# Attention over two batches as one program: the second batch's input and the first batch's output are normalised in pieces beside the pairs

## The chip, the cores and the metric

The kernel runs on one core of one Trainium2 chip. The metric is the device time of one execution in microseconds (us). A core has five engines that run their own instruction streams and wait for each other on semaphores: TensorE (PE; its weight loads are listed as PEld), VectorE (DVE), ScalarE (ACT), GpSimd (POOL), and SyncE (SP), which here only issues DMAs.

## The reference, cut to what matters

Two batches of 2048 tokens with 128 channels pass through four layers, each followed by `layernorm(x + layer(x))`: a state-space layer, a quantised linear layer, attention, and a mixture of experts. The change is in the third:

```python
mu = jnp.mean(latents, axis=-1, keepdims=True)
var = jnp.mean((latents - mu) ** 2, axis=-1, keepdims=True)
x = (latents - mu) * jax.lax.rsqrt(var + 1e-05) * ln_gamma + ln_beta
q = (x @ Wq) ...; k = (x @ Wk) ...; v = (x @ Wv) ...      # 16 heads of 64
scores = jnp.einsum('bhqd,bhkd->bhqk', q * scale, k * scale)
weights = jax.nn.softmax(scores, axis=-1)
out = jnp.einsum('bhqk,bhkd->bhqd', weights, v)
return out @ Wo
...
x = _layernorm(x + _L1_attn_ref(x, ...), axis=-1)
```

No token of one batch attends to the other batch, so the batches are independent.

## The kernel before, in words

`phase1` (the first two layers), `phase2` (attention) and `phase3` (experts) run one after the other. `phase2` runs four programs for batch 0 and then the same four for batch 1, with a barrier of all engines behind each:

- `attention_input` loads the 2048 tokens, normalises them (statistics on DVE, roots on ACT, scaling on both), turns them on PE (L951, 16 transposes of 128x128) and leaves them in `xaT` with gamma and beta applied.
- `attention_first` makes keys, queries and values of the first pair of heads, and the row maxima of its first scores.
- `attention_pairs` is the long one. Heads are taken in 8 pairs, queries in 4 chunks of 512. A **group** `g` is one pair and one chunk (32 groups per batch; `GC`), and its 16 key tiles are **units** `(g, kt)`. Groups are cut in 4 **turns** of 4 units (`TURNS`, `TURN`).
- `attention_output` finishes the last group, turns `attnT` back to tokens (L1493), adds the residual, normalises and stores.

Per unit in `attention_pairs`: PE computes two heads' scores in four terms (L1249) into one of two double banks; ACT takes their exponential into one of ten buffers `p` (`weigh`, L1356, `LIVE = 10`); PE multiplies them with the values (`values`, L1262); POOL adds up the denominators (L1389, 15 adds of 128x1024 per group, each waiting for the one before). ACT may fill a buffer of `p` again only when both PE and POOL have read what it held ten units earlier. Beside that, PE computes raw scores of groups ahead (L997), of which DVE takes row maxima (L1441) for the softmax shift. Only the group's last raw scores decide its shift (L1011 to L1013, turned by L1021, copied by ACT at L1329).

Each turn has two places for a further job, `USES_AT`, before and behind its four `values` steps: projections of the pair ahead, the denominator (`den`), the output projection (`out`), the shift. The place behind turn 3 is free:

```python
USES_AT = {(0, "before"): 0, (0, "behind"): "values", (1, "before"): "den", (2, "before"): "out",
           (2, "behind"): "shift", (3, "before"): 1}
```

A job's result lies in one of three banks used in turn (`TURNING`), shared with the raw scores. The third item behind a job waits until ACT (for a job behind) or DVE (before) has read it. At a turn's start ACT reads what was made behind the turn before; at turn 0 it then copies the finished group out of PSUM (`copy_outputs`, L1347, once per group), and takes four exponentials.

Jobs for the pair ahead exist only while there is one: in the last four groups of a batch there are no projections, and in the last two none or fewer raw scores.

## Time and profile before

| what | value |
|---|---|
| median of 3 runs | 3673.57 us (3668.96 to 3675.05) |
| the profiled execution's own time | 3673.23 us |
| its span, first to last instruction | 3671.3 us |
| busy, share of the span: PE | 3307.6 us, 90% |
| PEld | 1789.2 us, 49% |
| DVE | 2405.5 us, 66% |
| ACT | 1717.1 us, 46% |
| POOL | 2757.9 us, 75% |
| granted TensorE clock, mean | 0.954 of full speed |

An engine's share is a mean over stages that have different limits. A query for a stretch gives the same numbers for that stretch alone. In a timeline row the columns are start, duration, engine, line, operation, output<-inputs, count, and in brackets the idle time of the engine before it with what ended it.

### The profile page before, as it was taken

To read this page: it belongs to the slowest core of one execution; us is meant where nothing else is said; L and a number is where in the kernel's file an instruction comes from. 1 tells how busy PE (TensorE), PEld (TensorE's weight loads), DVE (VectorE), ACT (ScalarE), POOL (GpSimd) and SP (SyncE) were. 2 spreads that over 40 slices of the span, in tenths; PEclk is the share of its full clock that TensorE was granted. 3 is DMA by queue.
4 is the path that set the end of the run, shared out by engine and by line. 5 is a ranking of instruction groups with operands and counts; after the bars stand their busy time and mean duration, and the time that the engine had idled before them with its cause. 6 is when DMAs were issued, how large, how long until landed. Compare 5 with 4: busy or idle time off the path is not lost. (4 is left out here: it accounts for less than half of the span.)

```text
span 3671.3 us, 52128 instructions
## 1 busy us (share of the span) xinstructions
PE 3307.6 (90%) x19957; PEld 1789.2 (49%) x19957; DVE 2405.5 (66%) x3711; ACT 1717.1 (47%) x2081; POOL 2757.9 (75%) x1153
## 2 busy tenths in 40 slices
PE   5776587479999999999999499999999999997898
PEld 2223232245555555555555255555555555553798
DVE  5898599766666666666664466666666666663554
ACT  3331433135555555555555245555555555553554
POOL 1784088249998998998999378998998998997233
PEclk9898789789999999999999799999999999999999
DMA  1331133110000000000000100000000000000000
GB/s 25 132 109 35 47 128 109 30 44 1 4 1 4 1 4 4 1 4 1 2 1 1 41 3 1 4 4 1 4 1 4 1 4 2 1 1 12 27 18 15
DMA packets 61411, 76.31 MB, mean 21 GB/s; under 512 B 7274, under 2 KB 48820, under 8 KB 61108
## 3 DMA queue, kind: packets, MB, share of 16 engines
q1 hardware_dynamic: 59362, 72.71, 6.1%
q8 instruction: 156, 2.56, 0.3%
q14 instruction: 83, 0.68, 0.1%
q10 hardware_dynamic: 1810, 0.37, 0.0%
HBM read 66.24 MB, written 6.82 MB: 20 GB/s over the span
## 5 line engine op out<-in xcount | busy, mean ns | idle before, releaser
L1389 POOL TENSOR_TENSOR den_g<-den_g,p 128x1024 f32<-128x1024 f32 x896 | 2133.8, 2381 | 222.4 <-ACT p L1356 109.5
L1441 DVE TENSOR_REDUCE quarters<-psum 128x1 f32<-128x512 f32 x1960 | 1262.1, 686 | 732.0 <-PE psum L997 679.3
L1356 ACT ACTIVATE p<-psum 128x1024 f32<-128x1024 f32 x1024 | 1025.2, 1026 | 502.4 <-PE psum L1249 470.9
L1262 PE MATMUL psum<-p,v 128*64 128x512 f32 x4096 | 923.3, 593 | 0.0
L1262 PEld LDWEIGHTS psum<-p,v 128*64 128x64 f32 x4096 | 292.2, 137 | 579.3 <-issue 569.5
L997 PE MATMUL psum<-k_main,q_main 64*128 64x512 f32 x2048 | 438.7, 423 | 13.7 <-DVE quarters L1004 11.1
L1249 PE MATMUL psum<-q_main,k_main 64*128 64x512 f32 x2048 | 436.1, 421 | 7.1 <-PEq L1137 4.9
L1249 PE MATMUL psum<-q_rest,k_main 64*128 64x512 f32 x2048 | 407.4, 393 | 0.0
L1249 PE MATMUL psum<-q_main,k_rest 64*128 64x512 f32 x2048 | 407.0, 392 | 0.0
L1249 PE MATMUL psum<-row_shift,row_ones 64*128 64x512 f32 x2048 | 406.7, 391 | 0.0
L736 POOL TENSOR_TENSOR seen<-state,c_sb 128x2048 f32<-128x2048 f32 x64 | 285.4, 4461 | 68.5 <-DVE state L683 60.3
L997 PEld LDWEIGHTS psum<-k_main,q_main 64*128 64x128 f32 x2048 | 206.0, 185 | 222.0 <-issue 136.7
L621 PE MATMUL psum<-seen,ident 128*128 128x512 f32 x512 | 264.5, 654 | 27.2 <-POOL seen L736 27.0
L1249 PEld LDWEIGHTS psum<-q_main,k_main 64*128 64x128 f32 x2048 | 193.5, 185 | 167.1 <-ACT p L1356 128.4
L1249 PEld LDWEIGHTS psum<-row_shift,row_ones 64*128 64x128 f32 x2048 | 194.9, 185 | 44.5
L1249 PEld LDWEIGHTS psum<-q_main,k_rest 64*128 64x128 f32 x2048 | 194.5, 185 | 44.8
L1249 PEld LDWEIGHTS psum<-q_rest,k_main 64*128 64x128 f32 x2048 | 194.6, 186 | 11.5
L723 POOL TENSOR_TENSOR xnT<-dx,work 128x1024 f32<-128x1024 f32 x32 | 75.3, 2352 | 158.3 <-DMA work<-bc_rows 158.3
L1389 POOL TENSOR_TENSOR den_g<-p 128x1024 f32<-128x1024 f32 x64 | 152.4, 2381 | 46.6 <-ACT p L1356 46.6
L1329 ACT CAST row_shift<-psum 2x512 fp32r<-2x512 f32 x124 | 71.5, 577 | 243.5 <-PE psum L1021 242.0
L621 PEld LDWEIGHTS psum<-seen,ident 128*128 128x128 f32 x512 | 95.9, 201 | 153.3 <-issue 103.6
L1846 POOL TENSOR_TENSOR mixed<-mixed,part 128x512 f32<-128x512 f32 x56 | 74.1, 1324 | 104.2 <-DVE part L1811 104.2
(260 smaller groups left out, 3327.0 us busy)
## 6 DMA issues: line engine op xcount, KB each, us to landing
c_sb<-bc_rows SPq DMA_DIRECT2D x64, 512.0 KB, 3.5
work<-bc_rows SPq DMA_DIRECT2D x32, 512.0 KB, 4.9
resid<-in_resid SPq DMA_DIRECT2D x8, 256.0 KB, 3.6
x_mid<-resid SPq DMA_DIRECT2D x8, 256.0 KB, 2.6
xa<-x_mid SPq DMA_DIRECT2D x8, 256.0 KB, 3.7
x_tok<-x_mid SPq DMA_DIRECT2D x8, 256.0 KB, 3.8
x_mid<-x_tok SPq DMA_DIRECT2D x8, 256.0 KB, 2.7
x<-x_mid SPq DMA_DIRECT2D x8, 256.0 KB, 2.8
```

The lines of the kernel that those rows point to most:

```text
L621: last = nc.tensor.matmul(y_sum[:, h, k * BANK:(k + 1) * BANK], ident[:], seen[:, i % SLOTS, h, k * BANK:(k + 1) * BANK], start=False, sto ...
L723: nc.gpsimd.tensor_tensor(fed[:, k % SLOTS, :], dx[:, 1, s * SCAN:(s + 1) * SCAN], b_sb[:, k % SLOTS, :], ALU.mult).then_inc(fed_by_pool, 1)
L736: nc.gpsimd.tensor_tensor(seen[:, i % SLOTS, 0:halves], state[:, i % SLOTS, 0:halves], c_sb[:, i % C_SLOTS, :].unsqueeze(1).to_broadcast([ ...
L997: last = nc.tensor.matmul(to[h], q[hi(h), c * BANK + j * P:c * BANK + (j + 1) * P], k[hi(h), piece(quarter)], start=True, stop=True)
L1249: last = nc.tensor.matmul(s_bank(u)[:, piece(h)], left[hi(h)], right[hi(h)], start=(i == 0), stop=(i == len(terms) - 1))
L1262: last = nc.tensor.matmul(o_bank[hi(h), :], vv[:, kt, hi(h)], p[:, u % LIVE, h, :], start=(kt == 0), stop=(kt == KT - 1))
L1329: nc.scalar.copy(row_shift[at:at + 2, (g + 1) % 2, :], bank[at:at + 2, :]).then_inc(shift_read, 1)
L1356: nc.scalar.activation(flat(p[:, u % LIVE]), s_bank(u), ACT.Exp, scale=float(DH) ** -0.5).then_inc(p_ready, 1)
L1389: nc.gpsimd.tensor_tensor(sums, first, src, ALU.add).then_inc(added_g, 1)
L1441: nc.vector.reduce_max(quarters[:, to % 2, h, n:n + 1], bank_of["max", u, h], X_AXIS).then_inc(max_read, 1)
L1846: nc.gpsimd.tensor_tensor(mixed[:, u % 2], x[:, u % 2] if e == 0 else mixed[:, u % 2], part[:, e % 2], ALU.add).then_inc(summed, 1)
```

## The change

`attention_pairs` now runs once, for 64 groups of both batches (`GC` = 64, `NEXT` = 32 is the first group of batch 1). The programs `attention_output` of batch 0, `attention_input` of batch 1 and `attention_first` of batch 1 are gone, with the barriers between them. `xaT` holds both batches, and the projections and raw scores for batch 1's first pair become ordinary jobs of groups 28 to 31. What the three programs computed besides is done in eight pieces of 512 tokens: four `input` pieces (batch 1) with the statistics in groups 22 to 25, and four `output` pieces (batch 0) with the statistics in groups 31 to 34. The loads of the tokens stand on SP ahead of all weight loads. Among the jobs, `input` and `output` first stand in the code of PE (transposes behind turn 3), then in that of ACT (the read at the next turn's start); `rough_root` and `normalise_tokens` are ACT's at the end of turn 2, `variance`, `refine` (six operations on 128x4, each waiting for the one before) and `add_residual` POOL's, `statistics` DVE's at the end of turn 0. Core of the diff:

```diff
+    ALL_PAIRS = BATCH * PAIRS
+    GC, NEXT = ALL_PAIRS * CHUNKS, PAIRS * CHUNKS
+    batch_of = lambda g: g // NEXT
+    jobs = [("input", c, NEXT - 10 + c) for c in range(CHUNKS)] + [("output", c, NEXT - 1 + c) for c in range(CHUNKS)]
+    job_at = {start: j for j, (_, _, start) in enumerate(jobs)}
...
+            if (i % TURNS, place) == (TURNS - 1, "behind"):
+                if NEXT - 9 <= g < NEXT - 9 + CHUNKS:
+                    uses.append(("input", g - (NEXT - 9), i, place))
+                elif NEXT - 3 <= g < NEXT - 3 + CHUNKS:
+                    uses.append(("output", g - (NEXT - 3), i, place))
...
+                for c in range(CHUNKS):
+                    sp.dma_start(tok[:, c], tokens(x_in, 1, c)).then_inc(x_loaded, 16)
+                for c in range(CHUNKS):
+                    sp.dma_start(residual[:, c], tokens(x_in, 0, c)).then_inc(residual_loaded, 16)
...
+                    if pair == PAIRS:
+                        for c in range(CHUNKS):
+                            sp.wait_ge(tok_normed, CHUNKS + c + 1)
+                            sp.dma_start(tokens(x_out, 0, c), tok[:, c]).then_inc(stored, 16)
...
+                    if what == "input":
+                        pe.wait_ge(tok_normed, g + 1)
+                        for j in range(TPC):
+                            last = nc.tensor.transpose(bank[:, j * P:(j + 1) * P], tok[:, g, j, :], ident[:])
+                    elif what == "output":
+                        pe.wait_ge(freed_by_vector, freed(use_of["out", NEXT - CHUNKS + g]))
+                        for j in range(TPC):
+                            last = nc.tensor.transpose(bank[:, j * P:(j + 1) * P], attnT[:, (g * TPC + j) * P:(g * TPC + j + 1) * P], ident[:])
...
+                    elif what == "input":
+                        nc.scalar.activation(xaT[:, 1, piece(g)], bank, ACT.Identity, scale=gamma[:, 0:1], bias=beta[:, 0:1]).then_inc(freed_by_scalar, 1)
+                    elif what == "output":
+                        nc.scalar.copy(tok[:, g].rearrange("p t d -> p (t d)"), bank).then_inc(tok_copied, 1)
+                        act.wait_ge(tok_copied, g + 1)
+                        nc.scalar.nop().then_inc(freed_by_scalar, 1)
...
+                def rough_root(j):
+                    var, root = (factors[:, j, k, :] for k in range(2))
+                    act.wait_ge(var_ready, j + 1)
+                    nc.scalar.activation(root, var, ACT.Ln).then_inc(rough, 1)
+                    act.wait_ge(rough, 2 * j + 1)
+                    nc.scalar.activation(root, root, ACT.Exp, scale=-0.5).then_inc(rough, 1)
+                def normalise_tokens(j):
+                    act.wait_ge(refined, j + 1)
+                    c = jobs[j][1]
+                    for t in range(TPC):
+                        last = nc.scalar.activation(tok[:, c, t, :], tok[:, c, t, :], ACT.Identity, scale=factors[:, j, 1, t:t + 1],
+                                                    bias=factors[:, j, 3, t:t + 1])
+                    last.then_inc(tok_normed, 1)
...
+                def variance(j):
+                    pool.wait_ge(stats_done, j + 1)
+                    nc.gpsimd.tensor_scalar(factors[:, j, 0, :], two_t[:, j, :, 1], EPS, None, ALU.add).then_inc(var_ready, 1)
+                def refine(j):
+                    var, root, t, offset = (factors[:, j, k, :] for k in range(4))
+                    pool.wait_ge(rough, 2 * (j + 1))
+                    st.link(nc.gpsimd.tensor_tensor(t, root, root, ALU.mult))
...
+                    nc.gpsimd.tensor_scalar(offset, offset, -1.0, None, ALU.mult).then_inc(refined, 1)
...
+                def add_residual(c):
+                    pool.wait_ge(tok_copied, c + 1)
+                    pool.wait_ge(residual_loaded, 16 * CHUNKS)
+                    nc.gpsimd.tensor_tensor(tok[:, c], tok[:, c], residual[:, c], ALU.add).then_inc(tok_added, 1)
...
+                    if kt == 6 and g in job_at:
+                        variance(job_at[g])
+                    if kt == 1 and g - 1 in job_at:
+                        refine(job_at[g - 1])
+                    if kt == 4 and NEXT - 2 <= g < NEXT - 2 + CHUNKS:
+                        add_residual(g - (NEXT - 2))
...
+                def statistics(j):
+                    for t in range(TPC):
+                        last = nc.vector.bn_stats(six_t[:, t, :], tok[:, c, t, :])
+                    last.then_inc(stats_step, 1)
+                    dve.wait_ge(stats_step, j + 1)
+                    for t in range(TPC):
+                        last = nc.vector.bn_aggr(two_t[:, j, t, :], six_t[:, t, :])
+                    last.then_inc(stats_done, 1)
```

**PE, where the batches met.** Before, PE had these rows between batch 0's last values (`p_0`) and batch 1's first raw scores; the branches are ends of programs, where the barriers stand:

```order
L1262 MATMUL psum<-p_0,v 64x512 x8
L1197 UNCONDITIONAL_BRANCH
L1482 UNCONDITIONAL_BRANCH
L1485 MATMUL psum<-den_g,ones 64x512 x2
L1493 MATMUL psum<-ident,attnT 128x128 x12
L1490 MATMUL psum<-o_raw,w_o 128x512
L1493 MATMUL psum<-ident,attnT 128x128 x4
L1471 UNCONDITIONAL_BRANCH
L945 UNCONDITIONAL_BRANCH
L951 MATMUL psum<-ident,xa_1 128x128 x16
```

Of the change, the same engine at the end of turn 3 of group 32, the last of the four `output` pieces; L1031 is the job before the values, L1293 the values, L996 and L1280 the next group's raw scores and scores:

```order
L1031 MATMUL psum<-xaT,w_qkv 64x512 x2
L1293 MATMUL psum<-p,v 64x512 x8
L1309 MATMUL psum<-ident,attnT 128x128 x4
L996 MATMUL psum<-k_main,q_main 128x512 x2
L1280 MATMUL psum<-q_main,k_main 128x512 x2
```

The 16 transposes of `xa` and the 16 of `attnT` moved from the stretch between the batches to eight places of four, each behind the values of turn 3.

**ACT, in a group with an input piece.** Of the change, group 23 from the exponentials of turn 2 on (L1402 is before's L1356, L1375 its L1329, L1393 its L1347):

```order
L1402 ACTIVATE p<-psum 128x1024 x4
L1408 ACTIVATE factors<-factors 128x4
L1410 ACTIVATE factors<-factors 128x4
L1417 ACTIVATE tok<-tok,factors 128x128 x4
L1375 CAST row_shift<-psum 2x512 x2
L1402 ACTIVATE p<-psum 128x1024 x4
L1382 CAST q_main<-psum 128x512
L1367 ACTIVATE xaT<-psum,beta,gamma 128x512
L1393 COPY o_raw<-psum 128x512
```

Before, the row of L1329 stood directly behind that of L1356, and that of L1347 directly behind the cast of `q_main`: the three rows on `factors` and `tok` and the one on `xaT` are new there.

**POOL, in group 32 or 33, where most of it comes together.** Of the change (L1480 is before's L1389):

```order
L1480 TENSOR_TENSOR den_g<-p 128x1024
L1454 TENSOR_TENSOR factors<-factors 128x4
L1455 TENSOR_TENSOR factors<-factors 128x4
L1456 TENSOR_SCALAR factors<-factors 128x4
L1457 TENSOR_TENSOR factors<-factors 128x4
L1458 TENSOR_TENSOR factors<-two_t,factors 128x4
L1459 TENSOR_SCALAR factors<-factors 128x4
L1480 TENSOR_TENSOR den_g<-den_g,p 128x1024 x3
L1465 TENSOR_TENSOR tok<-tok,residual 128x512
L1480 TENSOR_TENSOR den_g<-den_g,p 128x1024 x2
L1448 TENSOR_SCALAR factors<-two_t 128x4
L1480 TENSOR_TENSOR den_g<-den_g,p 128x1024 x9
```

Before, a group was one row of `den_g<-p` and one of `den_g<-den_g,p` x14: seven operations on 128x4 and one on 128x512 now stand between its adds.

## Rows read from the trace of the kernel before

**Rows 1.** The page's busy time by engine.

```profile
PE 3307.6 (90%) x19957; PEld 1789.2 (49%) x19957; DVE 2405.5 (66%) x3711; ACT 1717.1 (47%) x2081; POOL 2757.9 (75%) x1153
```

**Rows 2.** Stretches: length, busy (count) of PE, PEld, DVE, ACT, POOL, clock, DMA share, GB/s.

```profile
829.00:1893.62 1064.62, 1064.59 (x7130) 561.89 (x7132) 691.85 (x1107) 560.34 (x649) 964.72 (x406) 1.00 0.01 2
1893.62:2034.34 140.72, 139.59 (x892) 71.04 (x892) 70.03 (x109) 72.38 (x81) 131.77 (x57) 1.00 0.00 1
2034.34:2120.71 86.37, 33.10 (x188) 17.07 (x188) 51.71 (x133) 21.78 (x44) 14.38 (x8) 0.72 0.15 43
```

**Rows 3.** Timeline of ACT: the copy that ends groups 0, 27, 31, 32.

```profile
829.00 0.59 ACT L1347 COPY o_raw<-psum 128x512 f32<-128x512 f32 x1 [2.85 <-PE psum L1262]
...
1893.62 0.59 ACT L1347 COPY o_raw<-psum 128x512 f32<-128x512 f32 x1 [2.85 <-PE psum L1262]
...
2034.34 0.58 ACT L1347 COPY o_raw<-psum 128x512 f32<-128x512 f32 x1 [2.56 <-PE psum L1262]
...
2162.97 0.59 ACT L1347 COPY o_raw<-psum 128x512 f32<-128x512 f32 x1 [2.85 <-PE psum L1262]
```

**Rows 4.** Timelines of PE, POOL and DVE at the join.

```profile
2030.64 3.65 PE L1262 MATMUL psum<-p,v 128*64 128x512 f32 x16
2045.05 1.97 PE L1485 MATMUL psum<-den_g,ones 128*64 128x512 f32 x4 [10.76 <-PEq L1457]
...
2082.52 3.55 PE L951 MATMUL psum<-ident,xa 128*128 128x128 f32 x16 [29.41 <-DVE xa L121]
...
2009.11 34.95 POOL L1389 TENSOR_TENSOR den_g<-den_g,p 128x1024 f32<-128x1024 f32 x14
...
2075.32 3.19 DVE L104 BATCH_NORM_STATS2 six<-xa 128x6 f32<-128x128 f32 x16 [11.94 <-DMA xa<-x_mid]
```

**Rows 5.** Timeline of PE: the first matmul of turns 1, 2, 3 of a group.

```profile
1233.58 0.50 PE L997 MATMUL psum<-k_main,q_main 64*128 64x512 f32 x2
...
1243.17 0.51 PE L997 MATMUL psum<-k_main,q_main 64*128 64x512 f32 x2
...
1252.98 0.50 PE L997 MATMUL psum<-k_main,q_main 64*128 64x512 f32 x2
```

**Rows 6.** Timeline of PE in the experts: four transposes, what follows.

```profile
3519.31 0.60 PE L1617 MATMUL psum<-ident,x 128*128 128x128 f32 x4
3519.75 1.95 PE L1660 MATMUL psum<-down_w,hid 128*128 128x128 f32 x16
```

**Rows 7.** Timeline of POOL in the same group.

```profile
1225.69 9.95 POOL L1389 TENSOR_TENSOR den_g<-den_g,p 128x1024 f32<-128x1024 f32 x4 [1.53 <-ACT p L1356]
1236.15 25.13 POOL L1389 TENSOR_TENSOR den_g<-den_g,p 128x1024 f32<-128x1024 f32 x10 [0.52 <-ACT p L1356]
```

**Rows 8.** Groups of POOL: count, busy us, mean ns.

```profile
L1044 POOL TENSOR_TENSOR q_rest<-raw,q_main 128x512 fp32r<-128x512 f32 x8 | 10.2, 1272 | 86.2 <-ACT raw L1110 86.2
L159 POOL TENSOR_TENSOR stat<-stat,exponent 128x4 f32<-128x4 f32 x8 | 8.2, 1021 | 5.4 <-DVE stat L1770 4.6
```

**Rows 9.** DVE: one timeline row, two groups, one line's min/median/max ns.

```profile
1234.12 2.68 DVE L1441 TENSOR_REDUCE quarters<-psum 128x1 f32<-128x512 f32 x4 [3.42 <-PE psum L997]
...
L104 DVE BATCH_NORM_STATS2 six<-x_tok 128x6 f32<-128x128 f32 x32 | 7.0, 280 | 0.3
L1011 DVE TENSOR_REDUCE maxima<-quarters 128x8 f32<-128x32 f32 x64 | 11.4, 178 | 0.1
...
L1013 DVE TENSOR_TENSOR shift<-maxima,shift x64: 195/769/2278, 777.3 to 3326.4; 128x8 bf16<-128x8 f32 x64
```

**Rows 10.** ACT: two timeline rows of turn 3, two of before's normalisation.

```profile
1253.09 1.18 ACT L1329 CAST row_shift<-psum 2x512 fp32r<-2x512 f32 x2 [3.94 <-PE psum L1021]
...
1257.03 1.94 ACT L1356 ACTIVATE p<-psum 128x1024 f32<-128x1024 f32 x2 [0.40 <-PE psum L1249]
...
2060.08 0.22 ACT L153 ACTIVATE stat<-stat 128x16 f32<-128x16 f32 x1
2061.37 3.18 ACT L131 ACTIVATE x_tok<-x_tok,stat 128x128 f32<-128x128 f32 x8 [1.08 <-DVE stat L118]
```

More of the change, by code:

```diff
@@ L1286, in use @@
                             pe.wait_ge(weights, 48 * (g // CHUNKS))
-                        last = project(nc, bank, w, xaT, projection(what, g))
+                        last = project(nc, bank, w, xaT[:, batch_of(g + CHUNKS)], projection(what, g))
                     last.then_inc(use_full, 1)
@@ L1455, in _ @@
                         make_shift(nc, st, quarters[:, (g + 1) % 2], maxima[:], shift).then_inc(shift_ready, 1)
+                    if i % TURNS == 0 and g in job_at:
+                        statistics(job_at[g])
                 dve.wait_ge(freed_by_vector, sum(place == "before" for *_, place in uses))
```

57 lines of the change are left out of this document (41 added, 16 removed).

## The prediction

> **What bounds the kernel now.** I read the page's busy time first: PE is busy in 90% of the span, POOL in 75%, no other engine in more than 66% [rows 1]. Then the same by stretch. From the end of group 0 to the end of group 27 PE works 1064.59 of 1064.62 us at a granted clock of 1.00, POOL 964.72 [rows 2]. That is the attention proper, and PE bounds it. The reader should see that the stretch between the batches is another thing: in 86.37 us PE works 33.10 and is granted 0.72 of its clock [rows 2], which is a mean over stretches at the 2.4 and at the 1.2 GHz level. So I looked for what stands there and for how long a group takes elsewhere.
>
> ACT copies each group out once, at a fixed place, so those copies are a ruler. Group 0's starts at 829.00 and group 27's at 1893.62: 27 intervals of 39.43 us [rows 3]. The last four groups of the batch take 2034.34 - 1893.62 = 140.72, or 35.2 each, since they have no pair ahead to prepare. Then 128.63 us pass until group 32, the first of batch 1, is copied at 2162.97 [rows 3].
>
> The timelines show the chain in between. PE finishes its values at about 2034.3, but POOL still adds until 2009.11 + 34.95 = 2044.06, and the next program's first matmul is at 2045.05. Batch 1's statistics start at 2075.32 behind an 11.94 us wait for a load, and its first transposes at 2082.52 behind 29.41 us without PE work [rows 4]. It is all latency in series: no engine is full.
>
> **The sum, made against the profiled execution's 3673.23 us** (span 3671.3 and 1.93 around it; the median of the runs, 3673.57, is 0.34 more).
>
> *Removed.* From group 27's copy to group 32's: 2162.97 - 1893.62 = 269.35 us [rows 3]. In the changed kernel this is five ordinary groups, since each now has the next pair to prepare: 5 x 39.43 = 197.15. The difference is **72.20 us**. It is less than the 89.20 us that the one interval across the join loses (128.63 - 39.43), because groups 28 to 31 grow from 140.72 to 157.72: the first pair's projections and raw scores of batch 1 move into them at PE's full rate.
>
> *Transposes on PE.* 32 transposes are no longer in the removed stretch but in eight places of four. Four of them between other matmuls put the next one 0.44 us later in the experts (3519.31 to 3519.75) [rows 6]. As a check on such a place: turn 1, with nothing behind its values, takes 1243.17 - 1233.58 = 9.59 us, turn 2, with eight small matmuls there, 9.81 [rows 5]. The lower bound for a place is that 0.22. For the upper I take 1.0, twice the transpose price and a little, as if the switch from the values' matmuls and back cost as much again. I take 0.44, the same operation and shape: 8 x 0.44 = **3.5 us** (1.8 to 8).
>
> *ACT at turn 0.* It reads the piece (0.59 us, the time of the copy of the same shape [rows 3]) ahead of the group's copy and four exponentials. It sits idle 2.85 us ahead of that copy [rows 3], but waits there for the values, behind which the new transposes come. So the read does not go into that idle time but into the gap before the first exponential, which waits for PE's scores. PE's scores of a unit wait for the exponential two units before, so what ACT loses there PE loses. I think about 0.1 us per piece is left over, **0.8 us** for eight; from 0 to the whole read, 4.7.
>
> *ACT at the end of turn 2.* Two root steps (0.22 each [rows 10]) and four scalings (eight take 3.18, so four 1.6 [rows 10]): 2.0 us in groups 23 to 25 and 32 to 34, less in the others. ACT sits idle 3.94 us there, waiting for the shift [rows 10]. Hidden, at nothing. Without that cover it would be 2.0 us a piece, 16 us; queued behind it are the shift's copy and the exponentials of turn 3, for which PE waits.
>
> *DVE.* Four statistics (mean 0.280) and four small aggregations, about 1.2 us by the rows' kind [rows 9], at the end of turn 0, where DVE sits idle 3.42 us until the first raw scores of turn 1 [rows 9]. Nothing.
>
> *POOL.* This is the engine that could come to bind. Ten adds take 25.13 us, 2.51 each with the wait for the one before; 15 are 37.7 of the 39.43 us, so 1.7 us are free per group [rows 7]. The change puts in up to seven operations on 128x4 and one on 128x512 (1.27 us [rows 8]). No row has a plain 128x4 operation on POOL. From below: 2.38 us for 1024 columns (2.51 less the wait of 0.13) and 1.27 for 512 give about 0.17 for none, with the wait 0.3. From above: the power on 128x4, 1.02 [rows 8], with the wait 1.15. It is a costlier function than a multiply, so I take the lower end: 7 x 0.3 + 1.4 = 3.5 us in the worst groups, 32 and 33. Less the free 1.7 POOL falls 1.8 us back in each, some 4 us over the output pieces, 1 over the input pieces. What may it fall back? The second exponential of the row at 1257.03, at about 1258.0, comes ten units after the one that the second add of the row at 1236.15 reads, so it fills the same buffer; that add is over at 1241.2, 17 us earlier [rows 7, 10]. So no wait of ACT on POOL: nothing.
>
> *DMAs on SP.* Eight loads of 256 KB ahead of the pair weights, four stores between two weight loads. At before's join four such loads had landed by 2075.32. A pair's weights are first used four groups, some 158 us, after their load is issued. Nothing.
>
> *A rule against the trace.* L1013, a DVE operation of 8 columns with two SBUF inputs, takes 195 ns at best and up to 2278; L1011 of the same place, with one SBUF input, has a mean of 178 [rows 9]. Beside POOL's adds the one kind is held up and the other not. The Trainium skill (SBUF — State Buffer, section Who interferes with whom) says why: a VectorE instruction with two SBUF inputs contends with a GpSimd one that reads SBUF, and the later waits for the whole of the other; with one SBUF input and outside the two-port modes it does not. By that rule the statistics, with one SBUF input, run free and the sum stays at 3605; if they were held up like L1013, the sum would be that of rival 3.
>
> **Sum:** 3673.23 - 72.20 + 3.5 + 0.8 = 3605.3, I say **3605 us**, 1.9% less. With the bounds above for transposes and reads: 3602.8 to 3613.7.
>
> **The rivals.**
>
> 1. *POOL's small operations cost what the power costs.* For: the only 128x4 row there is, 1.02 us [rows 8]. Against: the intercept of the adds. Then a group with variance and refinement has 8.05 us more work and 1.7 free, so POOL falls back about 6.3 us a group. ACT's root step waits for the variance, ready some 10 us ahead of it now (the add behind which it stands ends at 1238.7, ACT's turn 2 ends about 1249.2 by the 3.94 us idle before 1253.09 [rows 7, 10]). In the third input piece POOL is some 17 us late at that place; less 10 and less ACT's spare 2, ACT stops PE for 5 to 6 us, and in groups 33 and 34 again. About 18 us: **3623**. Chance 0.10.
> 2. *ACT's part of a piece is not hidden.* Read and end of turn 2 both push the exponentials: 0.59 + 2.0 = 2.6 us a piece, 8 pieces 21 us, less the 0.8 counted: **3625**. For: PE waits for exponentials all the time by a few tenths, and ACT had idle time only in pieces. Against: the 3.94 us. Chance 0.08.
> 3. *The statistics are held up by POOL's adds; this one ends slower.* Place: DVE, end of turn 0, with PE's raw scores waiting for DVE behind it. Price: each of eight operations waits out an add, 2.51 us: 20.1 + 1.2, less the cover of 3.4, is 17.9 a piece and 143 for eight: **3748**. At L1013's mean delay (a median of 0.77 against 0.195: 0.6) it is 8 x 0.6 + 1.2 - 3.4 = 2.6 a piece, 21 us and still a gain. It decides from 68 / 8 = 8.5 us a piece, 10.7 us over the eight, 1.3 us for each operation. For: L1013. Against: L1011. Chance 0.03 for slower, 0.02 for the mild form, about 3626.
> 4. *The join does not go away:* the new program waits at group 32 for something of batch 1 (a weight load, a piece of `xaT`), so that a good part of the 72 us comes back. Against: each piece is ready a full turn before PE asks for it, the last piece of `xaT` at turn 0 of group 27, a group ahead of the first projection. 30 us back would be **3635**. Chance 0.02.
>
> **How the numbers follow.** Forecast 0.75. The range takes in its bounds, 3602.8 to 3613.7, then the scatter of the three runs (about 3 us to either side), and reaches some way to rivals 1 and 2: 3600 to 3618; outside it I leave rivals 1 to 4 and little of the forecast, 2 in 10 or a bit more. Within 0.2% (7 us, about what a measurement of this kernel can tell from no change) nothing ends: 0.01. Slower 0.03, faster 0.96.
>
> **What the changed profile would show.** Copies of `o_raw` 39.4 us apart through groups 28 to 36, those with a piece at 39.9 to 40.0, a clock of 1.00 throughout. Four transposes in 0.4 us. DVE's statistics of 0.28 each and the first maximum of turn 1 not later than before against PE. POOL's 128x4 operations of 0.15 to 0.3 us; if they take 1 us, rival 1. ACT idle before L1375 down from 3.94 to about 2; if zero, rival 2. The forecast is wrong if intervals beside the pieces grow by more than 1 us, or if any interval between groups 27 and 36 stands out by itself.

## The result, and the profile after

The changed kernel's median is **3606.24 us** (four runs, 3603.16 to 3610.68), against 3672.99 (four runs, 3668.96 to 3675.05) for the kernel before: a ratio of **0.9821**, 95% interval 0.9803 to 0.9838. Its profiled execution took 3604.98 us, with a span of 3602.7. In a later comparison it was 3605.48 (five runs) against 3669.22 (nine), again 0.9821 [0.9806, 0.9835].

The page's busy time by engine answers to [rows 1]:

```profile
PE 3297.9 (92%) x19959; PEld 1785.3 (50%) x19959; DVE 2405.3 (67%) x3701; ACT 1723.8 (48%) x2110; POOL 2768.0 (77%) x1209
```

Every engine has about as much to do as before; the span around the work is what shrank. The stretches by engine (columns as in [rows 2]) run from group 0's copy to group 22's, on to group 27's (input pieces), from group 28's to group 33's (output pieces), and across the former join, 27 to 32:

```profile
829.29:1696.37 867.08, 866.97 (x5810) 457.51 (x5812) 565.27 (x910) 456.71 (x531) 786.09 (x332) 1.00 0.01 3
1696.37:1895.80 199.43, 199.41 (x1338) 105.50 (x1340) 132.26 (x229) 113.53 (x146) 183.77 (x103) 1.00 0.01 2
1935.23:2134.78 199.55, 199.53 (x1338) 105.40 (x1340) 135.60 (x229) 110.03 (x138) 184.66 (x95) 1.00 0.02 5
1895.80:2096.02 200.22, 200.21 (x1344) 106.19 (x1346) 133.38 (x222) 108.19 (x133) 183.63 (x87) 1.00 0.02 5
```

Across the join PE now works 200.21 of 200.22 us at a granted clock of 1.00. The 86.37 us stretch with 33.10 us of PE work and a clock of 0.72 [rows 2] has no counterpart. The ruler, that is ACT's copy of a finished group [rows 3], on the changed kernel's timeline, groups 0, 22, 27, 32 and 33:

```profile
829.29 0.59 ACT L1393 COPY o_raw<-psum 128x512 f32<-128x512 f32 x1 [2.85 <-PE psum L1293]
...
1696.37 0.59 ACT L1393 COPY o_raw<-psum 128x512 f32<-128x512 f32 x1 [2.85 <-PE psum L1293]
...
1895.80 0.59 ACT L1393 COPY o_raw<-psum 128x512 f32<-128x512 f32 x1 [2.85 <-PE psum L1293]
...
2096.02 0.59 ACT L1393 COPY o_raw<-psum 128x512 f32<-128x512 f32 x1 [0.17 <-ACT tok L1369]
...
2134.78 0.59 ACT L1393 COPY o_raw<-psum 128x512 f32<-128x512 f32 x1 [2.85 <-PE psum L1293]
```

From group 27's copy to 32's are 200.22 us where 269.35 stood. All intervals, read off the same copies in both traces:

| intervals (us) | before | after |
|---|---|---|
| mean of groups 0 to 22 | 39.43 | 39.41 |
| 22 to 27, each | 39.42, 39.44, 39.45, 39.46, 39.38 | 40.69, 39.97, 40.03, 40.00, 38.74 |
| 27 to 28 | 36.89 | 39.43 |
| 28 to 33, each | 36.72, 35.92, 31.19, 128.63, 39.41 | 40.79, 39.99, 40.02, 39.99, 38.76 |
| last copy to the end | 302.72 | 302.57 |

The first interval with a piece is longer and the one behind the last shorter for a reason of the ruler: ACT reads the piece ahead of the copy (`[0.17 <-ACT tok L1369]` in the row at 2096.02), so the mark itself moves. Over five intervals that cancels: 199.43 and 199.55 us, against 5 x 39.41 = 197.07. Four input pieces cost 2.4 us and four output pieces 2.5. In the first interval the growth is 1.28 us (40.69 - 39.41), of which 0.68 is the moved mark (ACT's read of the piece starts at 1776.35 in the rows below, the copy at 1777.03) and 0.60 the piece.

Where the 68.6 us of span went, by these marks: 69.1 gained between the copies of 27 and 32 (269.35 - 200.22), 2.3 lost to the input pieces (199.43 against 197.15 before), 0.65 gained in the interval from 32 to 33, which is 67.5; the other 1.1 is the ordinary group, shorter by some 0.02 us more than fifty times over, and the ends.

The four engines in a group with an input piece, one place each: PE's transposes and the first matmul of the next turn behind them; ACT at the end of turn 2 and its read at turn 0; DVE at the end of turn 0.

```profile
1775.66 0.66 PE L1304 MATMUL psum<-ident,tok 128*128 128x128 f32 x4
1776.24 0.50 PE L996 MATMUL psum<-k_main,q_main 64*128 64x512 f32 x2
```

```profile
1762.15 0.19 ACT L1408 ACTIVATE factors<-factors 128x4 f32<-128x4 f32 x1
...
1762.49 1.63 ACT L1417 ACTIVATE tok<-tok,factors 128x128 f32<-128x128 f32 x4
...
1766.19 1.18 ACT L1375 CAST row_shift<-psum 2x512 fp32r<-2x512 f32 x2 [2.06 <-PE psum L1020]
...
1776.35 0.78 ACT L1367 ACTIVATE xaT<-psum,beta,gamma 128x512 f32<-128x512 f32 x1 [3.43 <-PE psum L1304]
1777.03 0.58 ACT L1393 COPY o_raw<-psum 128x512 f32<-128x512 f32 x1
1777.71 2.19 ACT L1402 ACTIVATE p<-psum 128x1024 f32<-128x1024 f32 x2
```

```profile
1743.75 0.86 DVE L1541 BATCH_NORM_STATS2 six_t<-tok 128x6 f32<-128x128 f32 x4
1744.64 0.38 DVE L1545 BATCH_NORM_AGGREGATE two_t<-six_t 128x2 f32<-128x6 f32 x4
1747.25 2.67 DVE L1555 TENSOR_REDUCE quarters<-psum 128x1 f32<-128x512 f32 x4 [2.23 <-PE psum L996]
```

Four transposes put the next matmul 0.58 us later (0.59 in the output piece at 2014.56). ACT's wait for the shift fell from 3.94 us [rows 10] to 2.06: it ends at PE's moment, not at ACT's. DVE's wait for turn 1's first raw scores fell from 3.42 [rows 9] to 2.23, also with PE arriving last. POOL, in group 32 (timeline) with the refinement, and the groups of its new operations:

```profile
2054.08 2.38 POOL L1480 TENSOR_TENSOR den_g<-p 128x1024 f32<-128x1024 f32 x1
2056.41 0.20 POOL L1454 TENSOR_TENSOR factors<-factors 128x4 f32<-128x4 f32 x1
2056.69 0.20 POOL L1455 TENSOR_TENSOR factors<-factors 128x4 f32<-128x4 f32 x1
...
2058.01 7.42 POOL L1480 TENSOR_TENSOR den_g<-den_g,p 128x1024 f32<-128x1024 f32 x3
```

```profile
L1454 POOL TENSOR_TENSOR factors<-factors 128x4 f32<-128x4 f32 x8 | 1.6, 201 | 0.0
L1448 POOL TENSOR_SCALAR factors<-two_t 128x4 f32<-128x4 f32 x8 | 1.8, 229 | 0.7
```

A plain 128x4 operation takes POOL 0.2 us, 0.28 from start to start. The power takes 1.02 on the same shape [rows 8]: that is a price of the function, not of the shape.

### The profile page after: what moved, and what is told of

Same layout as the page of the kernel before. It is cut to its first block and busy times, and to the rows that moved or that the text cites. A ratio compares the mean times of both kernels' runs of the same rounds, so it can differ in the third digit from the quotient of the medians.

```text
span 3602.7 us, 52147 instructions
## 1 busy us (share of the span) xinstructions
PE 3297.9 (92%) x19959; PEld 1785.3 (50%) x19959; DVE 2405.3 (67%) x3701; ACT 1723.8 (48%) x2110; POOL 2768.0 (77%) x1209
## 5 line engine op out<-in xcount | busy, mean ns | idle before, releaser
L1480 POOL TENSOR_TENSOR den_g<-den_g,p 128x1024 f32<-128x1024 f32 x896 | 2133.6, 2381 | 216.1 <-ACT p L1402 105.2
L1555 DVE TENSOR_REDUCE quarters<-psum 128x1 f32<-128x512 f32 x2004 | 1290.7, 686 | 730.2 <-PE psum L996 677.7
L1402 ACT ACTIVATE p<-psum 128x1024 f32<-128x1024 f32 x1024 | 1025.3, 1026 | 476.7 <-PE psum L1280 443.3
L1293 PE MATMUL psum<-p,v 128*64 128x512 f32 x4096 | 922.9, 592 | 0.0
L1293 PEld LDWEIGHTS psum<-p,v 128*64 128x64 f32 x4096 | 293.3, 137 | 582.0 <-issue 577.0
L996 PE MATMUL psum<-k_main,q_main 64*128 64x512 f32 x2048 | 435.2, 420 | 6.8 <-DVE quarters L1003 5.5
L1280 PE MATMUL psum<-q_main,k_main 64*128 64x512 f32 x2048 | 434.1, 420 | 3.8 <-PEq L1136 2.7
L1280 PE MATMUL psum<-q_rest,k_main 64*128 64x512 f32 x2048 | 406.0, 392 | 0.0
L1280 PE MATMUL psum<-q_main,k_rest 64*128 64x512 f32 x2048 | 405.7, 391 | 0.0
L1280 PE MATMUL psum<-row_shift,row_ones 64*128 64x512 f32 x2048 | 405.0, 390 | 0.0
L996 PEld LDWEIGHTS psum<-k_main,q_main 64*128 64x128 f32 x2048 | 204.9, 184 | 205.1 <-issue 120.7
L1280 PEld LDWEIGHTS psum<-q_main,k_main 64*128 64x128 f32 x2048 | 192.8, 185 | 161.1 <-ACT p L1402 138.3
L1280 PEld LDWEIGHTS psum<-row_shift,row_ones 64*128 64x128 f32 x2048 | 194.1, 185 | 44.3
L1280 PEld LDWEIGHTS psum<-q_main,k_rest 64*128 64x128 f32 x2048 | 193.9, 185 | 44.0
L1280 PEld LDWEIGHTS psum<-q_rest,k_main 64*128 64x128 f32 x2048 | 194.4, 186 | 11.3
L1375 ACT CAST row_shift<-psum 2x512 fp32r<-2x512 f32 x126 | 72.7, 577 | 234.1 <-PE psum L1020 232.5
L1480 POOL TENSOR_TENSOR den_g<-p 128x1024 f32<-128x1024 f32 x64 | 151.9, 2374 | 23.6 <-ACT p L1402 23.6
```

The costliest lines, as they stand in the source:

```text
L996: last = nc.tensor.matmul(to[h], q[hi(h), c * BANK + j * P:c * BANK + (j + 1) * P], k[hi(h), piece(quarter)], start=True, stop=True)
L1280: last = nc.tensor.matmul(s_bank(u)[:, piece(h)], left[hi(h)], right[hi(h)], start=(i == 0), stop=(i == len(terms) - 1))
L1293: last = nc.tensor.matmul(o_bank[hi(h), :], vv[:, kt, hi(h)], p[:, u % LIVE, h, :], start=(kt == 0), stop=(kt == KT - 1))
L1402: nc.scalar.activation(flat(p[:, u % LIVE]), s_bank(u), ACT.Exp, scale=float(DH) ** -0.5).then_inc(p_ready, 1)
L1480: nc.gpsimd.tensor_tensor(sums, first, src, ALU.add).then_inc(added_g, 1)
L1555: nc.vector.reduce_max(quarters[:, to % 2, h, n:n + 1], bank_of["max", u, h], X_AXIS).then_inc(max_read, 1)
```

## The experiments

Each kernel is the changed one with the edit shown, unless said otherwise. The phases ahead of the attention end at another moment in each execution (the first copy at 826 to 833 us), so effects are read from the intervals between copies, and not from total times. Where the text gives an effect as a sum it is over the intervals from 22 to 36, against those of the changed kernel (556.58 us). Ordinary groups differ by up to 0.05 us from one execution to another (means of 39.39 to 39.45), so sums from first to last copy differ from these by up to 1.2 us. Each interval is read from one trace.

### The change without its pieces

The program over both batches stays, all eight pieces go. Batch 1's projections then read batch 0's tokens, and batch 0's output is its loaded input: those outputs are other numbers.

```
-    jobs = [("input", c, NEXT - 10 + c) ...] + [("output", c, NEXT - 1 + c) ...]
+    jobs = []
...
-                        last = project(nc, bank, w, xaT[:, batch_of(g + CHUNKS)], ...)
+                        last = project(nc, bank, w, xaT[:, 0], ...)
```

> The changed kernel without its eight pieces: one program for both batches, but nothing of batch 1's input or batch 0's output is normalised beside the pairs. Batch 1's projections read batch 0's tokens, and batch 0's output is stored as its unchanged input, so both outputs are other numbers; all pair work is there. My theory (the gain is the join's latency, the pieces cost only their transposes on PE, about 0.6 us each): all intervals between copies of o_raw from group 22 to 33 are 39.4, and the span is 4.8 us below the changed kernel's 3602.7, so about 3598, with no other stretch moved. Rival (the pieces are the reason for some other cost or saving, such as waits in later groups): the difference is not the sum of what the ten intervals beside the pieces show (2.4 + 2.5 us).

Measured: from group 0 to group 42 every interval is the ordinary one, 39.38 to 39.46, through the join too. The copies of groups 27 and 32:

```profile
1894.16 0.59 ACT L1390 COPY o_raw<-psum 128x512 f32<-128x512 f32 x1 [2.85 <-PE psum L1290]
...
2091.16 0.59 ACT L1390 COPY o_raw<-psum 128x512 f32<-128x512 f32 x1 [2.85 <-PE psum L1290]
```

2091.16 - 1894.16 = 197.00, so the one program is worth 269.35 - 197.00 = 72.35 us against the 72.20 forecast. Over the ten intervals 22 to 27 and 28 to 33 it is 197.13 and 197.04 against 199.43 and 199.55: there the pieces cost 4.8 us, 0.60 each. From first to last copy the difference is only 4.04 us (2466.80 and 2470.84), because behind group 33 this kernel took 0.93 us longer (1166.28 against 1165.35), with two intervals of 39.70 and 39.68; I did not look for their cause. The span, 3599.5 us, is 3.2 below the changed kernel's and not the 4.8 expected, since its first copy also came 0.77 us later. The gain and the cost of the change are now measured apart.

### The transposes twice

```
-                        for j in range(TPC):
+                        for j in range(2 * TPC):
+                            j %= TPC
```

in both `input` and `output` pieces.

> The changed kernel with each piece's four transposes done twice into the same bank, same result. Theory (a piece costs PE its transposes, 0.44 us for four, and 0.15 us for the change between kinds of matmul): 0.44 more a piece, 3.5 us over eight, intervals beside the pieces 40.4 instead of 40.0. Rival (the 0.6 us are latency around the piece, such as ACT's read, and the transposes are free): no change.

Measured: the intervals with pieces go from 40.0 to 40.40 to 40.47 (22 to 27: 41.08, 40.43, 40.47, 40.40, 38.74), 1.69 us over the four input pieces and 1.56 over the output pieces, or 0.41 a piece. At one place on PE's timeline (1778.06) eight transposes put the next matmul 1.02 us later, where four took 0.58: 0.44 for the second four. So four transposes among their own kind cost 0.41 to 0.44 us, about the experts' 0.44 [rows 6], and a place of four costs 0.60: 0.16 to 0.19 of each place belongs to having a place at all, behind the values and ahead of `k_main, q_main`. That the change of kind of matmul makes it is my reading, since nothing but PE's own stream is there; no run isolates it.

### POOL's small operations, more of them

POOL was the engine that I thought could come to bind, and rival 1 says how. The four links of the root's refinement run 6 and 10 times instead of once:

```
+                    for _ in range(6):     # the second kernel: range(10)
-                    st.link(nc.gpsimd.tensor_tensor(t, root, root, ALU.mult))
+                        st.link(nc.gpsimd.tensor_tensor(t, root, root, ALU.mult))
...
```

> The changed kernel with the four Newton steps of refine done six times on POOL (26 small operations for 6, each about 0.28 us with its wait, so 7.4 us for 1.7). This gives POOL per piece what rival 1 of the prediction supposed. Theory (POOL may fall back some 10 us before ACT's root step waits for the variance, and ACT then has 2 us to spare): nothing in the first two input pieces, then 3 us in the third, and about 5 us in the output pieces: 8 to 10 us over the changed kernel, span about 3612, with ACT's wait for POOL in front of the root step. Rival a (POOL's work beyond the 1.7 free us of a group is on the path at once): 6 us a piece, 45 us. Rival b (POOL has slack in plenty): 0.

> The same with ten times (42 small operations, 12.0 us a piece). Theory: once POOL is 10 us back, each further piece costs what it adds beyond the free time, about 9.5 us: 7 + 9.5 in the input pieces, 11 + 9.5 in the output pieces, some 37 to 50 us, span about 3640 to 3653. Rival a: 10 us for each of eight, 80 us. Rival b: 0.

Measured with 6: 17.0 us more than the changed kernel (4.4 up to group 28, 12.6 behind), and nothing in the first two pieces: 22 to 28 take 40.73, 40.00, 44.16, 39.99, 38.77, 39.63, and behind group 28 they take 40.74, 40.03, 40.05, 40.58, 46.69, 42.44, 39.41, 40.40. With 10: 52.5 us (20.1 and 32.4), a little above the 37 to 50 expected. The summary of waits of the first, from 1700 to 2300, and the place of the first stall on ACT's and on PE's timeline (a q behind an engine's name, as in ACTq, is its sequencer):

```profile
ACT factors L1408 <- POOL factors L1448: 20.2, 4, 7.8
```

```profile
1810.71 0.21 ACT L1408 ACTIVATE factors<-factors 128x4 f32<-128x4 f32 x1 [4.69 <-POOL factors L1448]
```

```profile
1813.86 0.51 PE L996 MATMUL psum<-k_main,q_main 64*128 64x512 f32 x2 [2.40 <-ACTq L1377]
```

That is rival 1's mechanism at its place: in two groups with both steps (23 and 24) POOL falls back unnoticed, in the third (25) ACT's root step waits for the variance that stands behind POOL's adds, and then PE waits for ACT. The variance comes 29.69 us behind the copy of group 24 (1810.45 and 1780.76), in the changed kernel 14.74 (1791.77 and 1777.03): POOL is 15 us late there, where the rival said some 17. The kernel has 27 x 0.28 = 7.6 us of small operations in such a group, near the rival's 8.05. The rival's price was 18 us, the run gave 17.0. That the totals come so close is partly luck: the rival had three stops of 5 to 6 us and no loss of clock, PE's stops were 2.40, 5.49 and 2.80 us, and the rest came behind them. For this run I had expected 8 to 10 us, less than the rival, and was wrong. One part that neither sum had is what comes behind the stall. The windows of the same kernel around it:

```profile
1811.06:1813.86 2.80, 0.40 (x5) 0.00 (x1) 0.56 (x1) 2.68 (x7) 2.66 (x2) 1.00 0.02 6
1813.86:1815.00 1.14, 1.14 (x8) 0.67 (x8) 0.59 (x1) 1.03 (x1) 1.14 (x1) 1.00 0.00 0
1815.00:1818.40 3.40, 3.40 (x20) 2.67 (x20) 1.98 (x4) 2.05 (x2) 3.11 (x3) 0.55 0.00 0
1820.00:1824.00 4.00, 4.00 (x22) 1.42 (x18) 1.20 (x2) 0.60 (x2) 3.71 (x3) 1.00 0.00 0
```

After PE had stood still for 2.40 us its granted clock was still 1.00 for the next 1.14, then 0.55 over 3.40 us, which is nearly all at the 1.2 GHz level, 0.89 over the next 1.60, and 1.00 again from 1820. At 0.55 of full speed those 3.40 us do the work of 1.9: the stall of 2.40 us cost another 1.5, together 3.9 of the 4.13 by which that interval grew. Not every stall was followed so. The one of 5.49 us was followed by 5 us at 0.50; the one of 2.80 us, in group 34 of the same kernel, by no loss at all:

```profile
2185.53 0.50 PE L996 MATMUL psum<-k_main,q_main 64*128 64x512 f32 x2 [2.80 <-ACTq L1377]
```

```profile
2185.53:2193.53 8.00, 8.00 (x48) 3.79 (x48) 4.56 (x7) 4.59 (x5) 7.57 (x4) 1.00 0.09 25
```

That interval grew by 3.06 us, hardly more than the stall.

In the kernel with 10 ACT's exponentials wait for a `p` buffer as well (`ACT p L1402 <- POOL den_g L1481`, 30.6 us in 24 waits from 1700 to 2300, none over 2.8), and with 6 a little (4.6 us in six). In the changed kernel that wait is 0.6 us in two, none over 0.4: the guard that the prediction counted, the ten buffers, is nearly whole there.

### Eight more DVE operations, with two and with one SBUF input

Rival 3 is about DVE beside POOL's adds. Eight operations on 128x8, with nothing else to wait for, stand ahead of each piece's statistics; in one kernel they have two SBUF inputs, in the other one.

```
+                    for k in range(8):
+                        extra.mark(nc.vector.tensor_tensor(scratch[:, k, :], ones[:, 0:8], ones[:, 8:16], ALU.mult))
+                    extra.wait()
                     for t in range(TPC):
                         last = nc.vector.bn_stats(six_t[:, t, :], tok[:, c, t, :])
```

The second has `nc.vector.tensor_reduce(scratch[:, k, 0:1], ones[:, 0:8], X_AXIS, ALU.max)` in that place.

> The changed kernel with eight more DVE operations of 8 columns with two SBUF inputs in front of each piece's statistics, written to a scratch tile that nothing reads. Theory by rival 3 of the prediction (such an operation waits out the POOL add that is running): if each of the eight waits for one add, 8 x 2.5 = 20 us, of which some 2 us are covered: 18 us a piece, up to 140 us in all; if only the first waits and the rest follow before POOL's next add, one wait of 0 to 2.4 us and eight times 0.1: 3 us or less, half covered, 0 to 1 us a piece. By L1013's mean delay of 0.6: 8 x 0.7 = 5.6, less 2.2 covered, 3.4 a piece, 27 us. Rival (operations of this size never wait): 1.0 us a piece more on DVE, inside the 2.2 us that are left, and no change of the time.

> The same as dve_two_inputs but with eight reductions of 8 columns, one SBUF input each. Theory (one SBUF input does not contend with POOL): 8 x 0.1 to 0.18 us, inside the 2.2 us that DVE has left at the end of turn 0; intervals as in the changed kernel, 0 us. Rival (statistics are held up by POOL as well, only short of the cover): durations scatter up to 2.4 us and the intervals beside the pieces grow.

Measured: one input, nothing (40.68, 40.00, 40.00, 40.00, 38.76, and 40.72, 40.01, 40.01, 40.02, 38.85). Two inputs, 17.9 us: 1.5 over the input pieces, then 40.72, 40.01, **45.96, 45.11, 43.64**, 39.89. One line of the kernel with two inputs (min, median and max in ns, first and last time), and DVE and POOL at one of the three places that cost most (the other two have the same 6.13 us, in the intervals 30 to 31 and 32 to 33):

```profile
L1545 DVE TENSOR_TENSOR scratch<-ones x64: 152/158/2346, 1666.2 to 2164.6; 128x8 f32<-128x8 f32 x64
```

```profile
2072.39 6.13 DVE L1545 TENSOR_TENSOR scratch<-ones 128x8 f32<-128x8 f32 x8
2078.55 0.87 DVE L1548 BATCH_NORM_STATS2 six_t<-tok 128x6 f32<-128x128 f32 x4
```

```profile
2067.46 7.45 POOL L1482 TENSOR_TENSOR den_g<-den_g,p 128x1024 f32<-128x1024 f32 x3 [1.07 <-ACT p L1404]
2074.88 1.28 POOL L1467 TENSOR_TENSOR tok<-tok,residual 128x512 f32<-128x512 f32 x1
2076.13 2.37 POOL L1482 TENSOR_TENSOR den_g<-den_g,p 128x1024 f32<-128x1024 f32 x1
```

Half of the 64 take 152 to 158 ns, some as long as one of POOL's adds. Eight in a row took 2.87 us beside each input piece and the last output piece, and 6.13 beside the other three output pieces: here one operation lasts until POOL's add ends (to 2074.9), one until the residual's add ends (2076.2) and one until the next add ends (2078.5), and the other five pass in between. The four statistics right behind, one SBUF input each, took 0.87 us, in the changed kernel 0.86. PE's wait for DVE behind that place, and the windows before and after it:

```profile
2080.56 0.50 PE L996 MATMUL psum<-k_main,q_main 64*128 64x512 f32 x2 [3.55 <-DVE quarters L1562]
```

```profile
2080.56:2083.00 2.44, 2.44 (x14) 2.24 (x16) 1.74 (x3) 0.65 (x1) 0.64 (x2) 0.58 0.00 0
2083.00:2085.00 2.00, 2.00 (x15) 1.84 (x13) 0.94 (x2) 0.89 (x2) 1.54 (x1) 0.66 0.00 0
2085.00:2087.00 2.00, 2.00 (x14) 0.79 (x12) 1.64 (x3) 1.78 (x3) 1.86 (x2) 1.00 0.00 0
```

3.55 us of stall, then 4.44 us at 0.58 and 0.66, that is 1.2 GHz for most of them: 1.7 us more. Together 5.2 us; the interval that it lies in, from 31 to 32, grew by 5.12. At all three places PE stood still for the same 3.55 us, yet the intervals grew by 5.94, 5.12 and 4.88: behind the first the clock was 0.50 for 5 us. The clock's share of such a loss is not fixed by the stall's length.

The rule that the prediction weighed (the Trainium skill, SBUF — State Buffer, section Who interferes with whom) holds in its direction: two SBUF inputs contend with POOL's reads, one does not, and the statistics belong to the second kind. The two kernels differ in the kind of operation too, a multiply and a reduction, but another line settles that: L1043, a TENSOR_TENSOR of 128x512 with one input in PSUM and one in SBUF, takes 690 to 692 ns in all its 117 instances beside POOL's adds in the changed kernel. So the SBUF inputs decide and not the operation. As a price the rule is too high if read as one add waited out per operation: eight waited out one to three of POOL's.

### ACT's part of a piece at other places of the turn

The root steps and scalings of turn 2 stand behind its last exponential. I held that ACT's 3.94 us of idle time there is what hides them. Two kernels do the same work earlier in the same turn, behind its second exponential and behind its first:

```
                     for u in range(i * TURN + LEAD_S, min((i + 1) * TURN + LEAD_S, len(units))):
                         weigh(u)
+                        if u == i * TURN + LEAD_S + 1:      # the other kernel: + LEAD_S
+                            ... rough_root(...), normalise_tokens(...)
-                    ... rough_root(...), normalise_tokens(...)
```

> The changed kernel with ACT's root step and scalings of a piece moved from the end of turn 2 to between the second and third of its four exponentials; same work, no idle time around it. Theory (at the end of turn 2 they are hidden in 3.9 us of idle time, without the cover they are on the path, since PE's scores wait for the exponential two units before): up to 2.1 us a piece where both steps stand together, six of them, 0.4 and 1.6 for the ones alone: 8 x 2.06 = 16 us, less what is left over, span 3612 to 3619. Rival (ACT has slack everywhere at 48% busy): 0.

> The changed kernel with ACT's root step and scalings of a piece between the first and the second exponential of turn 2. Between the second and third they cost nothing, which I had not expected. Theory now: the third and fourth exponential of a turn are needed only in the next turn, the first and second already by this turn's scores (those of unit n wait for the exponential of unit n - 2), so here a piece costs what ACT is late: 1.7 to 2.1 us where both steps stand together (six groups), 0.2 to 0.4 and 1.5 where one does, 11 to 16 us in all. Rival (PE has queued matmuls enough ahead of it, so that ACT's order within a turn does not matter): 0.

Measured behind the second: nothing (22 to 27: 40.64, 39.99, 39.98, 39.97, 38.74). My expectation fell. The rows of ACT there:

```profile
1803.11 1.03 ACT L1402 ACTIVATE p<-psum 128x1024 f32<-128x1024 f32 x1 [0.20 <-PE psum L1280]
...
1804.37 1.64 ACT L1417 ACTIVATE tok<-tok,factors 128x128 f32<-128x128 f32 x4
1805.91 1.91 ACT L1402 ACTIVATE p<-psum 128x1024 f32<-128x1024 f32 x2
...
1810.31 1.18 ACT L1375 CAST row_shift<-psum 2x512 fp32r<-2x512 f32 x2 [2.49 <-PE psum L1020]
```

The turn's third and fourth exponentials start late, and nobody minds; ACT then still waits 2.49 us for the shift, so the 3.94 us of idle time still take up most of the work, though it does not stand beside them. Measured behind the first: 42.21, 41.65, 41.56, 41.23, 38.78 for 22 to 27 and 5.9 us more behind 28, 11.9 in all, inside the 11 to 16 expected. There PE's next scores wait, while ACT's idle time ahead of the shift stays nearly whole (3.87 us in that group):

```profile
1803.17 0.50 PE L1280 MATMUL psum<-q_main,k_main 64*128 64x512 f32 x2 [1.36 <-ACT p L1402]
```

So idle time is half of the cover and position the other half: the gap takes up work put ahead of it only as long as nothing is pushed that PE asks for at once. That is the turn's second exponential (a place ahead of the first was not tried); the third and fourth are not missed before PE has gone on to the turn's values and the jobs behind them. Work of 2 us was free at both places tried behind the second, and cost about 1.5 us a piece between the first and it.

### The kernel before, with batch 1's tokens loaded early

If the join was latency in series, taking one link out must give that link back and no more. In the kernel before, the four loads of batch 1's tokens are issued during batch 0's pairs, into a tile of their own.

```
 def attention_pairs(...):
+                if b == 0:
+                    for c in range(CHUNKS):
+                        sp.dma_start(m["xa_pre"][:, c * TPC:(c + 1) * TPC, :], tokens(x_in, 1, c)).then_inc(...)
```

> The kernel before with one thing of the change: batch 1's tokens are loaded in batch 0's pairs program, so that attention_input of batch 1 waits for no load. Theory (the join is a chain of latencies, of which the load is one): DVE's statistics start 6 us earlier after the barrier; the load's 11.94 us wait began at the end of batch 0's scalings, before the barrier: about 6 us less than before, span about 3665. Rival (the statistics would have waited for something else, like the barrier or the table load): 0 to 2 us less.

Measured: the interval across the join is 120.85 us instead of 128.63, and the intervals behind are ordinary. DVE's first statistics:

```profile
2065.42 0.68 DVE L104 BATCH_NORM_STATS2 six<-xa_pre 128x6 f32<-128x128 f32 x3 [5.33 <-PEq L1531]
```

The wait for the load, 11.94 us [rows 4], has become one of 5.33 for the program's start: 6.6 of the 7.8 us, near the 6 expected. The other 1.2 lie behind batch 1's first scores. From the statistics to these it is 45.39 us in the kernel before and 45.49 here; from these to the copy of group 32, before and here:

```profile
2120.71:2162.97 42.26, 42.26 (x274) 24.43 (x276) 22.38 (x37) 22.31 (x24) 35.03 (x15) 0.93 0.02 6
...
2110.91:2151.94 41.03, 41.03 (x274) 23.11 (x276) 23.04 (x37) 22.33 (x24) 34.14 (x15) 0.96 0.02 6
```

PE does the same 274 matmuls without a gap in both, at a mean granted clock of 0.93 and 0.96: 3.0 and 1.6 us lost to it, which is the 1.2 within the rounding. So the link itself is worth 6.6 us, about a tenth of the join, and the rest is clock. The other links are read from the timeline and were not taken out one by one.

### A version that goes on

Behind the last pairs the changed kernel still has such a chain of its own: the output of batch 1 ends, then the experts' program loads its first tokens and PE waits for them. Here the first two of those loads are issued at the start of batch 1's output stage; for room, `newt` uses a part of `den_g` that is no longer needed.

```
 def attention_output(nc, x_in, x_out, b, m, experts):
+                for c in range(2):
+                    sp.dma_start(experts["x"][:, c], tokens(x_out, 0, c)).then_inc(experts["x_loaded"], 16)
```

> The changed kernel with one addition of the same kind: the first two loads of phase3 are issued in attention_output of batch 1 instead of at phase3's own start (batch 0's output is long in memory by then). PE's first transposes there now wait 2.7 us for the first load after the barrier. Theory (a join is a chain of latencies, and taking a load out of it takes out the wait for it): those transposes start 2 to 2.7 us earlier after the last group's copy, span and time 2 to 2.7 us below the changed kernel. Rival (something else ends at the same moment, such as the expert weights' splits): 0. Scatter of whole runs is 3 to 4 us, so the stretch from the last copy of o_raw to the end decides.

> The changed kernel unaltered, to compare with preload in the same rounds: 3606 us, 302.6 us from the last copy of o_raw to the end.

PE's first row of the experts, of the changed kernel repeated and then of the version with the early loads:

```profile
3338.93 0.47 PE L1733 MATMUL psum<-ident,x 128*128 128x128 f32 x1 [17.82 <-DMA x<-x_mid]
```

```profile
3333.47 0.45 PE L1735 MATMUL psum<-ident,x 128*128 128x128 f32 x1 [14.70 <-PEq L1644]
```

The wait is for the program now and no longer for a transfer, and it is 3.1 us shorter; 1.1 of that was lost ahead of it, where the output stage's last 3.97 us ran at a granted clock of 0.50 (2.85 us at 0.88 in the repeat). From the last copy of `o_raw` to these rows it is 37.10 us (from 3301.83) and 35.04 (from 3298.43), and to the end of the span 302.97 and 300.87: 2.1 us less, 1.7 against the first profile's 302.57. The medians, 3601.42 (five runs, 3595.58 to 3605.41) against 3605.48 (five, 3603.35 to 3607.24), go the same way, but the executions scatter by more than 2 us, and the profiled ones had their first copies 4 us apart before the edit could act (827.42 and 831.43). The gain in this stretch is read from one pair of traces; as a gain in time it is not shown.

## Why the prediction was right

Forecast 3605 us, measured 3606.2 and 3605.5; the profiled execution was 3604.98 against a sum of 3605.3. By its steps:

- **What bounds the kernel.** PE's stream in the pairs, and at the join a chain of latencies. Shown: without pieces the whole stretch runs at 39.4 a group, and one link of the old chain taken out gives back 6.6 us, with 1.2 of clock behind it. That the rest of the join is such links too is read from the timeline.
- **Removed, 72.20.** 72.35 measured by itself. The step that mattered was to compare 27 to 32 with five full groups and not the one long interval with one group, which would have said 89.
- **Transposes, 3.5.** Mis-sized: 0.60 a place and not 0.44, 4.8 us in all. The price of the transposes themselves was right (0.41 to 0.44); the place adds 0.16 to 0.19. The bounds of 0.22 to 1.0 a place held.
- **ACT's read at turn 0, 0.8.** Not seen. In the turn that begins at 1776.24 ACT's first exponential starts 1.47 us behind PE's first matmul of the turn (1777.71 and 1776.24), in a turn 0 without a piece in the trace of before 1.49 (1224.59 and 1223.10), and in an output piece 1.49 too (2016.64 and 2015.15). And the 0.60 a piece is what PE's stream alone explains (0.58 from the transposes to the next matmul), so nothing is left for the read. The two errors cancelled to 0.5 us. With the measured terms the sum is 3673.23 - 72.35 + 4.8 = 3605.7; that the forecast came within 0.3 us of the profiled execution is luck, as the four runs spread over 7.5 us.
- **ACT at turn 2.** Hidden as forecast, ACT's wait 2.06 where "about 2" was said. But the reason given, the idle time of 3.94 us at that place, is only half of it: the same work is as free two exponentials earlier, and three exponentials earlier it is not, though the idle time is there all the same. Rival 2's price of 2.6 us a piece holds nowhere: even at the worst place tried it is 1.5.
- **DVE.** Hidden, four statistics in 0.86 us. Rival 3's rule is real for another kind of operation; its top price of 143 us was far too high, with 18 us measured for eight operations a piece of the kind that contends, clock loss included. Its mild price, 21 us, is near that, but as 2.6 us at each of eight places, where 0.4 were measured at an input piece and 4.9 to 5.9 at three of the output pieces. The threshold of 8.5 us a piece for "slower" was not reached at any place.
- **POOL.** The small operations cost 0.28, forecast 0.3, and no wait of ACT for the variance is in the trace. Rival 1's mechanism is real: given 7.6 us of such work the kernel loses 17.0 us, beginning where it said, with POOL 15 us late where 17 was said. Between that and what the change does lie 5.6 us of POOL work a group.
- **DMAs, and the join coming back.** The clock is 1.00 from group 0 to group 33 and no part of the join came back: rival 4 did not happen. Of the prediction's own signs one was drawn too narrowly. Intervals beside pieces were to grow by no more than 1 us, and the first of each four grew by 1.28 and 1.38; the prediction had not seen that ACT's read moves its own ruler, by 0.68 and 0.75 us (2015.26 and 2016.01 in the output piece). Without that they grew by 0.60 and 0.63.

## What to carry to other kernels

Where the same work repeats, take one event a period as a ruler: a join costs what it is longer than the same number of full periods, and the pieces moved beside the work cost the growth of the intervals, to a few hundredths, where total times scatter by 3 us. Look whether the change moves the event itself. Work for an engine off the path is placed by what is asked for next and not by its idle time alone: here the same 2 us were free behind a turn's second exponential and cost 1.5 us behind its first, ahead of the same gap. A cheap piece can go beside full engines as long as each engine's backlog, counted over all the groups in a row that carry pieces, stays below what its reader waits for; price a stall on PE above its own length, since the clock may follow: by nothing up to 2.4 us for stalls of 2.40 to 5.49 us here.

## What of the hardware was unexpected

- **A short stall can cost a slow stretch behind it.** After 2.40 us without a matmul PE ran 3.40 us at a mean granted clock of 0.55, after 3.55 us 4.44 us at about 0.6, so mostly at the 1.2 GHz level with PE fully busy; after 1.36 us (the kernel with ACT's part behind the first exponential) the next 5.8 us were at 1.00. At the 2.40 us stall the clock fell 1.14 us after PE had resumed, not during it. The length of the stall does not settle it: after 2.80 us the next 8 us were at 1.00, and three stalls of the same 3.55 us cost 2.4, 1.6 and 1.3 us behind them.
- **Two SBUF inputs on DVE beside POOL's adds** are not an even tax: 152 to 158 ns for half of 64 operations and up to 2346 for single ones, which last until POOL's operation ends.
- **POOL's smallest operations are cheap:** 0.20 us for a multiply on 128x4 and 0.28 in a chain, where the power on the same shape takes 1.02 [rows 8].
